# Six rotated layers written out, each feed-forward inside the next attention's projections

## The reference, cut to what matters

```python
def attn_layer(x, Wqkv, qs, ksc, Wo):          # 16 heads of 64, windows of 32
    q, k, v = heads(x @ Wqkv)
    q = rotary(l2norm(q) * qs) ; k = rotary(l2norm(k) * ksc)
    return local_attention(q, k, v) @ Wo       # softmax over own and previous window

def ffn_layer(x, g, bln, W1, b1, W2, b2):
    mu = x.mean(-1, keepdims=True)
    var = ((x - mu) ** 2).mean(-1, keepdims=True)
    xn = (x - mu) / jnp.sqrt(var + 1e-05) * g + bln
    a, gate = jnp.split(xn @ W1 + b1, 2, -1)   # 341 columns each
    return a * jax.nn.gelu(gate, approximate=False) @ W2 + b2

for i in range(DEPTH):                         # DEPTH = 6
    x = attn_layer(shift_tokens(x), Wqkv[i], q_scale[i], k_scale[i], Wo[i]) + x
    x = ffn_layer(shift_tokens(x), ln_g[i], ln_b[i], W1[i], b1[i], W2[i], b2[i]) + x
```

## Time and profile before

| | |
|---|---|
| median of 3 runs | 2097.12 us (2096.36 to 2100.51) |
| the profiled execution's own time | 2112.46 us |
| its span, first to last instruction | 2110.7 us |
| PE busy / DVE busy | 1722.3 us (82%) / 1297.2 us (61%) |
| ACT busy / POOL busy | 881.1 us (42%) / 552.1 us (26%) |
| mean granted TensorE clock | 0.891 of full speed |
| stage F's first projection | starts at 1010.40 us |

### The profile page before, as it was taken

How to read it: one execution, slowest core, us unless ns; L and a number is a source line. 1 busy time by engine, 2 the same in 40 slices (tenths; PEclk the granted TensorE clock), 3 DMA queues, 4 the chain that set the end, 5 groups by cost and what they waited for, 6 DMA issues and landing times.

```text
span 2110.7 us, 42751 instructions
## 1 busy us (share of the span) xinstructions
PE 1722.3 (82%) x15585; PEld 903.0 (43%) x15585; DVE 1297.2 (61%) x2267; ACT 881.1 (42%) x1529; POOL 552.1 (26%) x524
## 2 busy tenths in 40 slices
PE   7884233189999999676799889989889998988998
PEld 2552111056565656222355354535535443553544
DVE  6664666656565656333767576566757656665674
ACT  2342111033434343322455454535544454554455
POOL 3350000000000000000445165244515525452551
PEclk9996555589999999777998999989998998999999
DMA  5120000100000000002321313131131313213130
GB/s 204 46 78 0 1 0 0 34 7 2 18 18 18 2 18 2 1 1 77 108 72 39 107 54 108 41 119 59 52 114 47 108 42 119 72 38 123 38 108 11
DMA packets 49279, 111.04 MB, mean 53 GB/s; under 512 B 15136, under 2 KB 19616, under 8 KB 47904
## 3 DMA queue, kind: packets, MB, share of 16 engines
q1 hardware_dynamic: 49056, 108.07, 15.6%
HBM read 28.61 MB, written 0.52 MB: 14 GB/s over the span
## 4 chain that ended last, share of the span: by engine, by line
issue 66%; POOL 15%; PE 10%; DVE 5%; ACT 2%; DMA 1%; POOLq 0%; DVEq 0%; ACTq 0%; SPq 0%
POOL big L567 4%; POOL big L559 4%; POOL big L560 4%; POOL big L552 2%; PE ps L324 2%; PE ps L384 1%; DVE big L501 1%; PE ps L367 1%; PE ps L353 1%; PE ps L394 1%; DVE big L530 1%; DMA big<-big 1%; DVE nm L527 1%; DVE big L500 1%; PE ps L345 0%
## 5 line engine op out<-in xcount | busy, mean ns | idle before, releaser
L559 POOL TENSOR_TENSOR big<-big 128x512 f32<-128x512 f32 x112 | 142.4, 1271 | 1274.8 <-DMA big<-big 1274.5
L567 POOL TENSOR_TENSOR big<-big,nm 128x384 f32<-128x384 f32 x224 | 184.3, 844 | 236.1 <-DVE nm L541 236.1
L471 ACT ACTIVATE big<-big 128x384 f32<-128x384 f32 x224 | 110.3, 523 | 217.8 <-DVE big L530 216.9
L500 DVE TENSOR_TENSOR big<-ps,big 128x512 f32<-128x512 f32 x224 | 153.6, 686 | 59.4 <-POOL big L560 37.2
L367 PE MATMUL ps<-ident,big 128*128 128x128 f32 x896 | 145.1, 298 | 28.5 <-POOL big L567 18.5
L324 PE MATMUL ps<-rs,big 32*128 32x512 f32 x384 | 118.9, 696 | 45.8 <-DVEq L168 20.2
L501 DVE TENSOR_TENSOR big<-ps,big 128x512 f32<-128x512 f32 x224 | 152.3, 680 | 0.0
L560 POOL TENSOR_TENSOR big<-big 128x512 f32<-128x512 f32 x112 | 142.7, 1274 | 0.0
L478 ACT ACTIVATE big<-ps 128x512 f32<-128x512 f32 x224 | 121.6, 585 | 50.3 <-PE ps L367 46.8
L1476 DVE TENSOR_TENSOR big<-ps,fix 128x512 f32<-128x512 f32 x192 | 119.1, 683 | 36.7 <-PE ps L1217 36.3
L527 DVE TENSOR_REDUCE nm<-ps 128x4 f32<-128x384 f32 x224 | 114.3, 552 | 43.6 <-PE ps L353 43.3
(11 more groups left out here) (262 smaller groups left out, 2998.1 us busy)
## 6 DMA issues: line engine op xcount, KB each, us to landing
big<-big SPq DMA_DIRECT2D x224, 256.0 KB, 2.4
big<-big SPq DMA_DIRECT2D x112, 128.0 KB, 2.4
big<-in_F_w SPq DMA_DIRECT2D x6, 1536.0 KB, 6.0
big<-big SPq DMA_DIRECT2D x84, 64.0 KB, 2.0
big<-in_D_w SPq DMA_DIRECT2D x12, 256.0 KB, 2.9
big<-in_F_wo SPq DMA_DIRECT2D x6, 512.0 KB, 7.1
big<-in_F_w SPq DMA_DIRECT2D x6, 341.0 KB, 3.1
big<-in_A_w SPq DMA_DIRECT2D x1, 1536.0 KB, 9.9
```

Of the source, the lines that this page charges most:

```text
L500: dve.tensor_tensor(tmp[:, i, w, :], ps[:, k, :], tb[:, 2 * w, :], ALU.mult).then_inc(*part.mark((key, b, p, 0)))
L559: pool.tensor_tensor(Q[:, p, :], tmp[:, i, 0, :], swp[:, i, 0:T], ALU.add).then_inc(*roped.mark((key, b, p)))
L567: pool.tensor_tensor(v, v, nm[:, p % 3, 16 + 4 * h:20 + 4 * h].unsqueeze(2).to_broadcast([128, 4, KW]), ALU.mult)\
```

## The change

The hardware loop over the layers is gone: six layers are written out in each queue, and every semaphore value is a constant. `attn_pe`, `attn_act` and `attn_dve` get hooks in place of `between`: a dictionary `early`, called after pair p of the projections, and `late`, called in the pair loop. By them the feed-forward of one sample and layer (`f_before` says which) runs in the next attention: that of sample 0 in sample 1's, and that of sample 1 in the attention of sample 0 one layer on. The feed-forward of the last sample of the last layer is written behind the loop.

The mean and its subtraction become one matmul with a centring matrix (identity less 1/128, a constant loaded into `fix`), whose result stays in bank 6 until DVE scales it there. The feed-forward has banks 6 and 7 during the projections: the centred values and then the three gate products go to bank 6, the variance and then the three up products to bank 7. The down product goes to bank 2 in the pair loop. Its buffers lie in `fix`, `xc` and half of `rs`. V's blocks, which used banks 4 and 6 in turn, now use bank 4, and bank 6 for the blocks 5 and 7 only (`v_bank`), in stage A too. The scaled tables are made in the pair loop of sample 1, a layer ahead. SP loads Wqkv of the next layer at the end of a layer's transfers, Wo at the head of its own layer once the last L545 has run, and the feed-forward's weights before the transfers of sample 1. PE waits for both attention weights before a layer's first projection.

```diff
+        def v_bank(i):
+
+            return 6 if i in (5, 7) else 4
+
         def a_v_pe(pe, key, b, src, i):
-            kv = 4 + 2 * (i % 2)
-            if i < 2:
+            kv = v_bank(i)
+            if i in (0, 5):
                 take(pe, kv)
             else:
-                pe.wait_ge(*v_ready.at((key, b, i - 2)))
+                pe.wait_ge(*v_ready.at((key, b, i - 1 if i < 5 else i - 2)))
...
-        def attn_pe(pe, key, src, l2, between={}):
-            for b in range(B):
-                a_proj_pe(pe, key, b, src(b), l2)
+        def attn_pe(pe, key, src, l2, hooks=lambda b: ({}, {})):
+            for b in range(B):
+                early, late = hooks(b)
+                a_proj_pe(pe, key, b, src(b), l2, early)
...
-                    if b == 1 and p in between:
-                        between[p]()
+                    if p in late:
+                        late[p]()
...
-            attn_pe(pe, "F", lambda b: xsh[:, b, :], True, {2: lambda: f_mean_pe(pe, 0, 2), 4: lambda: d_var_pe(pe, "F1", 0, 2)})
-            pe.wait_ge(ff_loaded, L * 80 + 80)
-            f_up_pe(pe, 0, 0)
-            f_mean_pe(pe, 1, 7)
-            f_up_pe(pe, 0, 1)
-            f_up_pe(pe, 0, 2)
-            d_var_pe(pe, "F1", 1, 7)
-            f_down_pe(pe, 0)
-            for i in range(3):
-                f_up_pe(pe, 1, i)
-            f_down_pe(pe, 1)
...
-            attn_act(act, "F", True, {3: lambda: f_square_act(act, 0, 2), 5: lambda: d_root_act(act, "F1", 0, 2), 7: norm_done})
-
-            f_gelu_act(act, 0, 0)
-            f_gelu_act(act, 0, 1)
-            f_square_act(act, 1, 7)
-            f_gelu_act(act, 0, 2)
-            act.preload_act_table_set("natural_log_exp_and_others")
-            d_root_act(act, "F1", 1, 7)
-            f_xn_act(act, 1)
-            for i in range(3):
-                f_gelu_act(act, 1, i)
-            act.preload_act_table_set("natural_log_exp_and_others")
...
-            attn_dve(dve, "F", True, {1: lambda: f_shift_dve(dve, 0), 3: lambda: f_centre_dve(dve, 0, 2), 6: lambda: d_scale_dve(dve, "F1", 0)})
-            f_shift_dve(dve, 1)
-            f_centre_dve(dve, 1, 7)
-            dve.wait_ge(ff_loaded, L * 80 + 80)
-            for b in range(B):
-                for i, (c0, m) in enumerate(DIC):
-                    k = up_bank[2 * i]
-                    dve.wait_ge(*full[k].at(("F", b, "f", k)))
-                    dve.wait_ge(*gg.at((b, i)))
-                    if b == 1:
-                        dve.wait_ge(*full[6].at(("F", 0, "f2")))
-                    dve.scalar_tensor_tensor(fh[0:m, i, :], ps[0:m, k, :], b1[0:m, i:i + 1], fg[0:m, i, :], ALU.add, ALU.mult)\
-                        .then_inc(*f_mul.mark((b, i)))
-                    read(dve, k, f_mul, (b, i))
-                if b == 0:
-                    d_scale_dve(dve, "F1", 1)
-                dve.wait_ge(*full[6].at(("F", b, "f2")))
-                dve.scalar_tensor_tensor(x[:, cols(b)], ps[:, 6, :], lng[:, 2:3], x[:, cols(b)], ALU.add, ALU.add).then_inc(*x_new.mark(("Ff", b)))
-                read(dve, 6, x_new, ("Ff", b))
-                shift_dve(dve, b, (moved, 1))
...
+        fsq, frs, fxn = xc[:, 0, :], rs[:, 0, :], xc[:, 1, :]
+        fg = (fix[:, N:N + T], fsq)
+        centre_f = fix[:, N + T:N + T + 128]
+        fh = fix[:, N + T + 128:N + 4 * T + 128].rearrange("p (i t) -> p i t", i=3)
...
+        def f_centre_pe(pe, l, b):
+            pe.wait_ge(*shifted.at((l, b)))
+            take(pe, 6)
+            pe.matmul(ps[:, 6, :], centre_f, xsh[:, b, :], start=True, stop=True).then_inc(*full[6].mark(("F1", l, b, "xc")))
+
+        def f_var_pe(pe, l, b):
+            pe.wait_ge(*squared.at(("F1", l, b)))
+            take(pe, 7)
+            pe.matmul(ps[:, 7, :], mean_m[:, :], fsq, start=True, stop=True).then_inc(*full[7].mark(("F1", l, b, "var")))
+
+        def f_up_pe(pe, l, b, i):
+            c0, m = DIC[i]
+            if i == 0:
+                f_ff_wait(pe, l)
+                pe.wait_ge(*affine.at(("F", l, b)))
+            take(pe, 6)
+            pe.matmul(ps[0:m, 6, :], W1[:, DI + c0:DI + c0 + m], fxn, start=True, stop=True).then_inc(*full[6].mark(("F", l, b, "gate", i)))
+            take(pe, 7)
+            pe.matmul(ps[0:m, 7, :], W1[:, c0:c0 + m], fxn, start=True, stop=True).then_inc(*full[7].mark(("F", l, b, "up", i)))
+
+        def f_down_pe(pe, l, b):
+            take(pe, 2)
+            for i, (c0, m) in enumerate(DIC):
+                pe.wait_ge(*f_mul.at((l, b, i)))
+                last = pe.matmul(ps[:, 2, :], W2[0:m, i, :], fh[0:m, i, :], start=i == 0, stop=i == 2)
+            last.then_inc(*full[2].mark(("F", l, b, "f2")))
...
+        def f_before(l, b):
+
+            return (l, b - 1) if b else (l - 1, B - 1) if l else None
+
+        def f_pe_hooks(pe, l, b):
+            u = f_before(l, b)
+            if u is None:
+                return {}, {}
+            return ({0: lambda: f_centre_pe(pe, *u), 2: lambda: f_var_pe(pe, *u), 4: lambda: f_up_pe(pe, *u, 0), 5: lambda: f_up_pe(pe, *u, 1),
+                     6: lambda: f_up_pe(pe, *u, 2)}, {1: lambda: f_down_pe(pe, *u)})
...
+            for l in range(LAYERS):
+                pe.wait_ge(fw_in, 16 * (l + 1))
+                pe.wait_ge(fwo_in, 16 * (l + 1))
+                attn_pe(pe, ("F", l), lambda b: xsh[:, b, :], True, lambda b, l=l: f_pe_hooks(pe, l, b))
+            u = (LAYERS - 1, B - 1)
+            f_centre_pe(pe, *u)
+            f_var_pe(pe, *u)
+            for i in range(3):
+                f_up_pe(pe, *u, i)
+            f_down_pe(pe, *u)
...
+        def f_square_act(act, l, b):
+            act.wait_ge(*full[6].at(("F1", l, b, "xc")))
+            act.activation(fsq, ps[:, 6, :], ACT.Square).then_inc(*squared.mark(("F1", l, b)))
...
+        def f_root_act(act, l, b):
+            act.wait_ge(*full[7].at(("F1", l, b, "var")))
+            act.activation(frs, ps[:, 7, :], ACT.Ln, bias=eps5[:, 0:1]).then_inc(*f_log.mark((l, b)))
+            read(act, 7, f_log, (l, b))
+            act.activation(frs, frs, ACT.Exp, scale=-0.5).then_inc(*rooted.mark(("F1", l, b)))
...
+        def f_xn_act(act, l, b):
+            f_ff_wait(act, l)
+            act.wait_ge(*normed.at(("F1", l, b)))
+            act.activation(fxn, fxn, ACT.Identity, bias=lng[:, 1:2], scale=lng[:, 0:1]).then_inc(*affine.mark(("F", l, b)))
+
+        def f_gelu_act(act, l, b, i):
+            m = DIC[i][1]
+            act.wait_ge(*full[6].at(("F", l, b, "gate", i)))
+            if i == 2:
+                act.wait_ge(*f_mul.at((l, b, 0)))
+            act.activation(fg[i % 2][0:m, :], ps[0:m, 6, :], ACT.Gelu, bias=b1[0:m, 3 + i:4 + i]).then_inc(*gg.mark((l, b, i)))
+            read(act, 6, gg, (l, b, i))
...
+        def f_act_hooks(act, l, b):
+            u = f_before(l, b)
+            if u is None:
+                return {}, {}
+
+            def last():
+                f_gelu_act(act, *u, 2)
+                f_exp_table(act)
+            return ({1: lambda: f_square_act(act, *u), 3: lambda: f_root_act(act, *u), 4: lambda: f_xn_act(act, *u), 5: lambda: f_gelu_act(act, *u, 0),
+                     6: lambda: f_gelu_act(act, *u, 1), 7: last}, {})
...
+        def f_scale_dve(dve, l, b):
+            dve.wait_ge(*rooted.at(("F1", l, b)))
+            dve.tensor_tensor(fxn, ps[:, 6, :], frs, ALU.mult).then_inc(*normed.mark(("F1", l, b)))
+            read(dve, 6, normed, ("F1", l, b))
+
+        def f_mul_dve(dve, l, b, i):
+            m = DIC[i][1]
+            dve.wait_ge(*full[7].at(("F", l, b, "up", i)))
+            dve.wait_ge(*gg.at((l, b, i)))
+            dve.scalar_tensor_tensor(fh[0:m, i, :], ps[0:m, 7, :], b1[0:m, i:i + 1], fg[i % 2][0:m, :], ALU.add, ALU.mult).then_inc(*f_mul.mark((l, b, i)))
+            read(dve, 7, f_mul, (l, b, i))
+
+        def f_add_dve(dve, l, b):
+            dve.wait_ge(*full[2].at(("F", l, b, "f2")))
+            dve.scalar_tensor_tensor(x[:, cols(b)], ps[:, 2, :], lng[:, 2:3], x[:, cols(b)], ALU.add, ALU.add).then_inc(*x_new.mark(("Ff", l, b)))
+            read(dve, 2, x_new, ("Ff", l, b))
...
+        def f_dve_hooks(dve, l, b):
+            u = f_before(l, b)
+            early, late = {}, {}
+            if u is not None:
+                early = {3: lambda: f_scale_dve(dve, *u), 5: lambda: f_mul_dve(dve, *u, 0), 6: lambda: f_mul_dve(dve, *u, 1), 7: lambda: f_mul_dve(dve, *u, 2)}
+                late = {1: lambda: f_add_dve(dve, *u), 2: lambda: shift_dve(dve, u[1], (moved, 1))}
+            if b == B - 1 and l + 1 < LAYERS:
+                late[4] = lambda: f_tab_dve(dve, l + 1)
+            late[NP + 2] = lambda: f_shift_dve(dve, l, b)
+            return early, late
...
+        def f_loads(sp, l, b):
+            if b == 0 and l > 0:
+                sp.wait_ge(*x_new.at((("F", l - 1), B - 1)))
+                f_wo_sp(sp, l)
+            if b == B - 1 and l > 0:
+                sp.wait_ge(*x_new.at(("Ff", l - 1, B - 1)))
+                f_ff_sp(sp, l)
...
```

(23 more changed lines are left out.)

219 lines of the change are left out of this document (84 added, 135 removed).

## The result

The changed kernel takes 2228.57 us (median of 4 runs, 2224.75 to 2229.68) against 2098.82 us (median of 4, 2096.36 to 2110.52) of the kernel before: ratio 1.0603, 95% interval 1.0561 to 1.0646. It is slower by 130 us at the median. Between the two profiled executions the span goes from 2110.7 to 2227.8 us, which is 117 us. The prediction had slower, and the waits, but put it at +73 on the same execution; 2228.57 lies above its range.

What follows compares the result with a forecast made beforehand. PE was taken to bound the projections, so added feed-forward matmuls and waits cost 16.6 us per half. With pair-loop, layer-head and other terms, +72.8 us on 2112.46 gave 2185, scaled to the median 2169 us; range 2110 to 2215.

Steps and rivals of the forecast that it cites:

- the "faster" rival: In the projections, ACT and DVE run ahead so PE never waits: about 2079 us, chance 0.12.
- gate 0: In the projections, PE's wait before the first gate product for gain and bias: 2.7 us idle per half.
- gate 1: In the projections, PE's wait before the second gate product for bank 6, freed by the first Gelu: 3.0 us.
- gate 2: In the projections, PE's wait before the third gate product for the second Gelu: 1.7 us idle.
- up 2: In the projections, PE's wait before the third up product for bank 7, freed by DVE: 0.65 us.
- the end: At the projections' end, inverse norms wait for the last Gelu and the Exp table: 0.95 us more than before.
- Wo: At a layer's head, PE idles until this weight's transfer lands: 4.7 us, up to 8.2.
- a drain beside the table loads: On ACT, about 1.38 us extra per table switch by the Trainium skill; time near 2199, chance 0.02.
- I add 1 us for that: 76 us: Half-layer without feed-forward: 75 us plus 1 us for the spread, part of it clock in a pair loop.
- a rival at 3 us a half with a chance of 0.17: In projections and heads, idle lowers PE's clock: 3 us for each of eleven halves, 2200 us, chance 0.17.
- the base half: Layer 0's sample 0, without feed-forward: 76.9 us less about 2 for first matmuls at half clock, so 75.
- the tables, 1.5 us: Table scaling moved into sample 1's pair loop, where DVE sets the pace: 1.5 us, bounds 0 to 1.7.

Runs made afterwards that it cites:

- Experiment 3: Changed kernel with the three gate and up products one pair later in PE's queue (behind pairs 5, 6, 7): 2080.82 us, ratio 0.9906.
- experiment 6: Changed kernel with Gelu replaced by Identity and no table loads in stage F (output not the reference's): 2155.7 us, ratio 1.0280.
- experiment 2: Changed kernel with PE's wait for Wo moved from the first projection to the output product: 2195.87 us, ratio 1.0456.
- experiment 7: Changed kernel with four unread matmuls before PE's wait for Wo at the head of layers 1 to 5: 2211.04 us, ratio 1.0528.
- experiment 1: Changed kernel with the next layer's table scaling behind pair 7 of sample 1's pair loop instead of pair 4: 2191.2 us, ratio 1.0430.
- experiment 8: Changed kernel with the four table multiplies spread one behind each of pairs 3 to 6, instead of all behind pair 4: 2189.45 us, ratio 1.0451.
- experiment 9: Changed kernel with two unread matmuls before the first gate product's wait, in eleven of twelve feed-forwards: 2215.26 us, ratio 1.0548.

## Why the prediction fell short

**Right: what would be lost, and to whom.** PE's own work and the order in ACT's queue decide; the "faster" rival (the waits are met in time) fell. The waits against their forecasts: gate 0 2.02 for 2.7, gate 1 2.73 for 3.0, gate 2 1.31 for 1.7, up 2 1.34 for 0.65, the end 0.87 more than before (2.02 for 1.15 in the earlier trace rows) for 0.95, Wo 4.1 for 4.7. They sum to 8.3 for 9.0 per half without Wo. Experiment 3 removed 92 us of idle where 99 was forecast. Nor was a drain beside the table loads to be seen (experiment 6).

**The step that failed: the clock.** The prediction put it as "I add 1 us for that: 76 us", a price per half taken over from the kernel before, and as a rival at 3 us a half with a chance of 0.17, kept apart from the waits that cause it. The new waits were summed at their length. Measured by experiment 3, eleven halves' waits cost 92 us of idle and 55 us of slower matmuls, so each us of wait brought 0.6 us more. The part of it in layer 1's projections is the seven matmuls in sample 0's projections at 0.85 us each, and two in sample 1's: 47.2 for 41.4 forecast, and 43.1 for 41.8. The rival was priced from a window's clock and from one row that lay before it: q behind 4.11 us of idle at 2.07 us. In the sum, the same row was subtracted from the base half as an accident of layer 0 and not carried to the five heads and eleven gates where the change puts idles of 2 to 4 us. Experiments 2 and 7 show the head's share twice: 2.4 and 2.6 us beside a wait, with the wait gone and with the wait filled.

**The second step: the tables, 1.5 us.** The bounds were 0 to 1.7, the upper one being all of the earlier trace rows's 1.67. Those rows are from a stretch in which POOL was idle. In the loop POOL works beside DVE, the four took 3.78 us, and the delay fell to the pair chain and the clock: a loop of 57.6 us against 52.7 in layer 5, which has no tables, so 4.9. (The forecast counted the term for layer 5 too.) Experiments 1 and 8 give back 37 and 39 us, 7 to 8 per layer, more than this, since half-clock stretches in the halves that follow go as well: half-clock time falls from 174.7 to 132.7 and 122.5, and in experiment 1 the projections of layer 1's sample 0 take 42.7 in place of 47.2 us.

**The balance, on the profiled execution.** Forecast +72.8. Layers: 203.7 for 195.4, five times +8.3, is +41.6 (sample 0's halves 103.7 for 99.1, sample 1's 100.0 for 96.3). Layer 0's second half +5.7. The end +1.9: gate 0 starts 7.9 us after L527 (forecast 8.0), the three rounds take 8.5 for 7.1, the first gate and up product at half clock (2.02 and 1.83 us), the rest 4.0 for 3.4. Layer 0's first half ended 3.6 us earlier than before: 3.0 of this are there when stage F's first projection starts (1007.39 for 1010.40 us), so they come from the stages in front, and why is open. Stage A's expected 1 us for V in one bank did not come (its last step starts at 161.44 and 161.46 us in the two kernels). These are -3.6 and -1. Together +117.4, against 117.1 of the span.

**The step from the profiled run to the median.** The profiled execution of before (2112.46) was above all its companions (2096.36 to 2100.51), so the forecast scaled it down by 0.7%. The changed kernel's profiled execution (2229.68) was within 1.2 us of its own median. The scaling made the forecast 16 us lower than the sum; that is a part of the miss of 60 at the median, and it was no mechanism.

**What stays open.** Why a given idle is followed by half clock in one place and not in another (4.05 and 4.00 us at the same head, experiment 9) is not settled. Nor is there one price. Over stage F, each us of idle that went took with it 0.6 us of PE's busy time in experiments 2 and 3, about 1.0 in experiments 1 and 8, and 1.6 in experiment 6. And the half-clock total alone does not give the time: in experiment 7 it stayed (173.2 us) while the kernel got 17.5 us faster, as half clock moved out of the projections into the pair loop (layer 1).

## What to carry to other kernels

When work is moved into the queue of a full PE, price each new wait at its length plus the matmuls at half clock behind it; here at least 0.6 us for each us of wait, and up to 1.6. Take the price from a row that shows a matmul behind an idle of that size, and do not set such a row aside as a start-up effect. And try each hook one slot later before giving it up: gate and up products asked for one slot too early cost 148 us in this kernel.
